# Order of tile 0's gating, of the scale's load and of the softplus chain in a fused adapter and feed-forward kernel

## The chip, the cores and the metric

The kernel runs on one core of one Trainium2 chip. The metric is device time in microseconds from the start to the end of one execution. The engines are TensorE (PE, its weight loads PEld), VectorE (DVE), ScalarE (ACT), GpSimd (POOL) and SyncE (SP); each works through its own list of instructions in order, and they meet through semaphores.

## What is computed

Two layers follow each other, and x is added at the end. Shapes: x is 128 x 32 x 512 in float32; E = 8 experts of rank R = 16.

```python
base    = einsum('btd,od->bto', x, W)
logits  = einsum('btd,ed->bte', x, Wr) + onehot(lang_ids) * 5.0
topw, topi = top_k(logits, 2);  weights = softmax(topw)
gates   = sum(onehot(topi) * weights[..., None], axis=-2)
h       = einsum('btd,erd->bter', x, A)
cond    = base + 2.0 * einsum('bter,bte,eor->bto', h, gates, B)
out     = x + einsum('bsi,io->bso', cond, sign) * softplus(scale)
```

The kernel folds the two layers into one matrix: M = W^T · sign · softplus(scale) + identity, and B2 = B · sign · 2·softplus(scale). Then out = x·M + (gated h)·B2.

## The kernel before

**Numbers in two parts.** Each float32 operand is split into a high part (rounded by a copy to the fp32r type) and a low part (the operand less its high part). A product is three matmuls: high·high, high·low, low·high. High parts are mostly ACT copies, low parts are subtractions on DVE or POOL.

**The start.** PE runs 18 warm-up matmuls (L577) and then M from W and sign, in four slices j of each (`high_high`, `low_high`, `high_low`, L589, L596, L603, the last slice at L569 to L571). The list of PE is fixed: `high_high(0)`, `low_high(0)`, `high_high(1)`, `high_low(0)`, and so on. `low_high(0)` waits for w_lo of slice 0. ACT issues the four loads of sign (L330), loads its function table (L332), and makes w_hi (L335) and sign_hi of slices 1 to 3 (L340). DVE makes sign_hi of slice 0 (L437) and all four w_lo (L422). POOL fills the identity blocks (L284) and makes all four sign_lo (L293). SP loads W, x of tile 0, the scale (L245), A, B, and x of tiles 1 and 2.

**Before the tiles.** DVE takes -|scale| (L443), transposes x of tile 0 (L432), and runs the rest of softplus as eight small dependent instructions (L448 to L457), between which ACT takes exp (L356) and ln (L358). Then come A and Wr transposed (L461, L464), m_full = p_m · softplus + eye (L470), and the low parts of the heads (Wr and A, L481 and L483) and of b (L487). PE makes p_b2 from b's parts (L626, L630); b2_hi is ACT's (L375), b2_lo is DVE's (L501, in `low_b2`).

**The tiles.** There are 32, one per time step, with three sets of buffers. For a tile, DVE transposes x (`turn_x`, L432), ACT makes xt_hi (`high_x`, L348), POOL makes xt_lo (`low_x`, L300), and PE multiplies them with `wide`, which holds the logits, the 128 columns of h, and M (L643; tile 0 at L668). DVE then gates: logits plus bias (L516), the largest (L524), their places (L532), a cast (L537), the denominator from ACT's exp (L540), `second` (L542), a reciprocal (L545), `gate` (L547) and h_gated (L551). PE transposes h_gated (`turn_h`, L686), ACT and DVE split it (ht_hi L381, ht_lo L507), and PE adds its product with b2 in the middle of a later tile's matmuls (`lora`, L679). The work is skewed: `step` s of PE multiplies tile s, adds the lora of tile s-2 in its middle, and ends with `turn_h` of tile s-1. In DVE's and ACT's step s the gating is of tile s-1, ht's parts are of tile s-2, and the transpose and the high part are of tile s+2. DVE's step 0 holds the transpose of x of tile 2 and then `low_b2`. In step 1 the transpose of tile 3's x (x3) stands in the middle of tile 0's gating, between the largest and their places, as it does in every later step.

Of the kernel before, what the change touches and what calls it, by code (L numbers as in the profile page):

```python
# [4 lines left out]
FP32 = mybir.dt.float32  # L5
# [7 lines left out]
P = 128  # L13
# [5 lines left out]
def adaln_ffn_kernel(nc: bass.Bass, x, lang_ids, W, Wr, A, B, sign, scale, out):  # L19
# [38 lines left out]
    with ctx:  # L58
# [138 lines left out]
        def slot(r, d=0):  # L197
            return (r + d) % S3
# [20 lines left out]
        def has(s, d):  # L219

            return s is None or 0 <= s + d < TILES

        @block.sync
        def _(sp_eng):
# [19 lines left out]
            load(0, 0, 0)  # L244
            sp_eng.dma_start(scale_in[:, :], scale.partition_broadcast(P)).then_inc(scale_loaded, 16)  # L245
            for i in range(NQ):
# [80 lines left out]
        def _(act):  # L327

            for j in range(OC):
                act.dma_start(sign_in[:, j, :], sign_load[:, j, :]).then_inc(sign_loaded[j], 16)  # L330

            nc.scalar.preload_act_table_set("natural_log_exp_and_others")  # L332
            for j in range(OC):
                act.wait_ge(w_loaded[j], 16)
                nc.scalar.activation(w_hi[:, j, :, :, :],  # L335
                                     w_in[:, j, :].rearrange("p (i k a) -> p k i a", i=NQ, k=KC),
                                     ACT.Copy).then_inc(w_hi_made, 1)
                if j >= EARLY:
                    act.wait_ge(sign_loaded[j], 16)
                    nc.scalar.activation(sign_hi[:, j, :], sign_in[:, j, :], ACT.Copy).then_inc(sign_hi_made, 1)  # L340

            def high_x(q, r, d, first=False):
# [9 lines left out]
            for i in range(NQ):  # L352
                act.dma_start(wr_in[Q * i:Q * i + E, :], wr_load[i, :, :]).then_inc(wr_loaded, 16)
            act.dma_start(ids_in[:, :], lang_ids.rearrange("(p a) -> p a", a=1)).then_inc(ids_loaded, 16)
            act.wait_ge(neg_abs_made, 1)
            nc.scalar.activation(exp_neg[:, :], sp[:, 0:1], ACT.Exp).then_inc(exp_neg_made, 1)  # L356
            act.wait_ge(exp_neg_made, 1)
            nc.scalar.activation(ln_one[:, :], exp_neg[:, :], ACT.Ln, bias=1.0).then_inc(ln_one_made, 1)  # L358
            high_x(0, 0, 0, first=True)
            act.wait_ge(head_turned, 1)  # L360
            nc.scalar.activation(wide_hi[:, :, E:HEAD].rearrange("p j (g b) -> p g j b", g=NQ), at[:, :, :, :],
                                 ACT.Copy).then_inc(head_hi_made, 1)
            act.wait_ge(head_turned, 2)
            nc.scalar.activation(wide_hi[:, :, 0:E], wrt[:, :, 0:E], ACT.Copy).then_inc(head_hi_made, 1)
            act.wait_ge(b_loaded, 16 * OC)
            nc.scalar.activation(b_hi[:, :, :, :], b_in[:, :, :, :],
                                 ACT.Copy).then_inc(b_hi_made, 1)
            for k in range(KC):
# [36 lines left out]
        def _(dve):  # L405
# [29 lines left out]
            for j in range(EARLY):  # L435
                dve.wait_ge(sign_loaded[j], 16)
                nc.vector.tensor_copy(sign_hi[:, j, :], sign_in[:, j, :]).then_inc(early_sign_hi_made, 1)  # L437
                low_w(j)
            for j in range(EARLY, OC):
                low_w(j)  # L440

            dve.wait_ge(scale_loaded, 16)
            nc.vector.tensor_scalar(sp[:, 0:1], scale_in[:, :], -1.0, scale_in[:, 0:1], ALU.mult, ALU.min)\  # L443
                .then_inc(neg_abs_made, 1)
            turn_x(0, 0, 0, first=True)

# [10 lines left out]
            nc.vector.tensor_scalar(sp[:, 11:12], sp[:, 10:11], SCALING, None, ALU.mult).then_inc(softplus_made, 1)  # L457
            softplus = sp[:, 10:11]

            dve.wait_ge(a_loaded, 16 * NQ)  # L460
# [12 lines left out]
            def low_m(k):  # L473
# [4 lines left out]

            fold(0)
            dve.wait_ge(head_hi_made, 2)  # L480
            nc.vector.tensor_tensor(wide_lo[:, :, 0:E], wrt[:, :, 0:E], wide_hi[:, :, 0:E].bitcast(FP32),  # L481
# [3 lines left out]
                                    ALU.subtract).then_inc(head_lo_made, 1)  # L485
            dve.wait_ge(b_hi_made, 1)
            nc.vector.tensor_tensor(b_lo[:, :, :, :], b_in[:, :, :, :],  # L487
                                    b_hi[:, :, :, :].bitcast(FP32), ALU.subtract).then_inc(b_lo_made, 1)
            fold(1)
# [7 lines left out]
            def low_b2():  # L497

                dve.wait_ge(bias_made, 1)
                dve.wait_ge(b2_hi_made, 1)  # L500
                nc.vector.scalar_tensor_tensor(b2_lo[:, :], p_b2[:, :], sp[:, 11:12], b2_hi[:, :].bitcast(FP32),  # L501
                                               ALU.mult, ALU.subtract).then_inc(b2_lo_made, 1)
# [7 lines left out]
            def step(q, r, s):  # L510
                done = S3 * q + r
                n = slot(r, -1)
                if has(s, -1):

                    dve.wait_ge(head_ready, done)
                    nc.vector.tensor_tensor(logits[:, :], pair[n][0][:, 0:E], bias[:, :], ALU.add)\  # L516
                        .then_inc(logits_made, 1)
                    dve.wait_ge(logits_made, done)
# [4 lines left out]
                if has(s, -1):  # L523
                    nc.vector.max(top[:, :], logits[:, :]).then_inc(top_made, 1)  # L524
                    dve.wait_ge(top_made, done)
                if s == 0:
                    turn_x(q, r, LEAD, first=True)
                    low_b2()
                elif has(s, LEAD):
                    turn_x(q, r, LEAD, first=(s is not None and s + LEAD < S3))  # L530
# [4 lines left out]
                if has(s, -1):  # L535
# [18 lines left out]
                        gate[:, :].unsqueeze(2).to_broadcast([P, E, R]), ALU.mult, ALU.mult)\  # L554
                        .then_inc(h_gated_made, 1)
                if s == TILES - 1 + LAG:

# [210 lines left out]
```

## Time and profile before

| | |
|---|---|
| time, median of 3 runs | 165.2 us (165.15 to 165.34) |
| time of the profiled execution | 164.64 us |
| its span, first to last instruction | 162.8 us |
| TensorE clock granted, mean share | 0.997 |
| busy: PE, DVE, ACT, POOL | 158.3, 97.6, 66.0, 52.1 us |

The profiled execution lies 0.56 us below the median of the runs, and 1.84 us of its time are outside its span. Positions below are microseconds from the start of the span. A timeline row gives start and length; a merged row (x4) gives the first start and the stretch to the last end. In brackets stands the idle time of the engine ahead of the row and what ended it. The names b_lo and pair stand for several tensors whose numbers are left out: b_lo at L501 is b2_lo.

### The profile page before, as it was taken

How to read it: one execution, taken by the hardware profiler on the slowest of the kernel's cores; microseconds unless marked ns; L12 is line 12 of the kernel's file. 1: busy time of each engine (PE TensorE's matmuls, PEld its weight loads, DVE VectorE, ACT ScalarE, POOL GpSimd, SP SyncE). 2: the span in 40 equal slices, each digit the busy share in tenths (PEclk: the TensorE clock that was granted, in tenths of full speed). 3: DMA queues.
4: the chain of work that ended last, by engine and by line, in shares of the span. 5: the costliest groups of instructions: out<-in, count | busy, mean ns of one | idle time of the engine just before them, and what ended most of it. 6: DMA issues, size and time to landing. Idle time of an engine off the chain costs nothing.

```text
span 162.8 us, 3711 instructions
## 1 busy us (share of the span) xinstructions
PE 158.3 (97%) x1070; PEld 153.8 (94%) x1070; DVE 97.6 (60%) x416; ACT 66.0 (41%) x177; POOL 52.1 (32%) x50
## 2 busy tenths in 40 slices
PE   7999998999999999999999999999999999999993
PEld 5788897999999999999999999999999999999992
DVE  5689997555556665554554555556665555455741
ACT  3654722434344333344444343344333344443440
POOL 2994453332222233333333322222333333333000
PEclk9999999999999999999999999999999999999998
DMA  4996323424333333334333333333333333111113
GB/s 170 380 146 136 90 82 101 131 70 146 105 122 114 124 119 115 124 129 129 129 129 127 104 101 117 112 121 123 113 123 120 128 129 129 64 64 64 68 66 129
DMA packets 29431, 19.51 MB, mean 120 GB/s; under 512 B 7248, under 2 KB 24432, under 8 KB 29424
## 3 DMA queue, kind: packets, MB, share of 16 engines
q1 hardware_dynamic: 28496, 18.23, 36.5%
q10 hardware_dynamic: 928, 1.20, 2.0%
q8 instruction: 3, 0.05, 0.1%
q14 instruction: 4, 0.03, 0.1%
HBM read 11.03 MB, written 8.39 MB: 119 GB/s over the span
## 4 chain that ended last, share of the span: by engine, by line
PE 90%; DVE 7%; issue 1%; ACT 0%; DVEq 0%
PE pair L643 66%; PE pair L679 14%; PE p_b L577 2%; PE p_ht L686 2%; PE pair L589 2%; DVE m_full L470 2%; PE pair L596 2%; PE pair L603 2%; DVE xt L432 1%; DVE wide_lo L476 1%; DVE gate L547 1%; DVE b_lo L501 0%; DVE b_lo L487 0%; DVE wide_lo L483 0%; ACT y L395 0%
## 5 line engine op out<-in xcount | busy, mean ns | idle before, releaser
L300 POOL TENSOR_TENSOR xt_lo<-xt,xt_hi 128x512 fp32r<-128x512 f32 x32 | 41.6, 1299 | 91.5 <-ACT xt_hi L348 91.5
L643 PE MATMUL pair<-wide_hi,xt_hi 128*128 128x392 f32 (+1 forms) x248 | 60.8, 321 | 0.0
L643 PE MATMUL pair<-wide_hi,xt_lo 128*128 128x392 f32 (+1 forms) x248 | 58.3, 311 | 0.0
L643 PE MATMUL pair<-wide_lo,xt_hi 128*128 128x392 f32 (+1 forms) x248 | 58.3, 311 | 0.0
L643 PEld LDWEIGHTS pair<-wide_hi,xt_lo 128*128 128x128 f32 x248 | 38.6, 188 | 0.0
L643 PEld LDWEIGHTS pair<-wide_lo,xt_hi 128*128 128x128 f32 x248 | 38.5, 188 | 0.0
L643 PEld LDWEIGHTS pair<-wide_hi,xt_hi 128*128 128x128 f32 x248 | 38.3, 189 | 0.1
L394 ACT ACTIVATE y<-pair 128x256 f32<-128x256 f32 x31 | 11.9, 384 | 44.3 <-PE pair L679 44.3
L516 DVE TENSOR_TENSOR logits<-pair,bias 128x8 f32<-128x8 f32 x32 | 5.3, 165 | 35.7 <-PE pair L643 35.7
L432 DVE STREAM_TRANSPOSE xt<-x_in 128x512 f32<-128x512 f32 x32 | 22.7, 710 | 3.7 <-DVE top L524 3.2
L348 ACT ACTIVATE xt_hi<-xt 128x512 fp32r<-128x512 f32 x32 | 20.3, 633 | 2.8 <-DVE xt L432 2.8
L381 ACT ACTIVATE ht_hi<-p_ht 128x128 fp32r<-128x128 f32 x32 | 8.9, 277 | 22.6 <-PE p_ht L686 22.6
L507 DVE TENSOR_TENSOR ht_lo<-p_ht,ht_hi 128x128 fp32r<-128x128 f32 x32 | 9.3, 290 | 13.6 <-ACT ht_hi L381 13.6
L385 ACT ACTIVATE e<-top 128x1 f32<-128x1 f32 x32 | 9.5, 296 | 14.4 <-DVE top L524 14.3
L551 DVE SCALAR_TENSOR_TENSOR h_gated<-pair,rdenom,gate 128x128 f32<-128x128 f32 x32 | 11.2, 350 | 3.3
L679 PE MATMUL pair<-b_hi,ht_hi 128*128 128x256 f32 x64 | 13.0, 281 | 0.0
L679 PE MATMUL pair<-b_lo,ht_hi 128*128 128x256 f32 x64 | 12.9, 280 | 0.0
L679 PE MATMUL pair<-b_hi,ht_lo 128*128 128x256 f32 x64 | 12.8, 279 | 0.0
L395 ACT ACTIVATE y<-pair 128x256 f32<-128x256 f32 x32 | 12.2, 380 | 1.4 <-PE pair L679 1.4
L679 PEld LDWEIGHTS pair<-b_hi,ht_hi 128*128 128x128 f32 x64 | 9.9, 188 | 0.1
L679 PEld LDWEIGHTS pair<-b_lo,ht_hi 128*128 128x128 f32 x64 | 9.9, 188 | 0.0
L679 PEld LDWEIGHTS pair<-b_hi,ht_lo 128*128 128x128 f32 x64 | 9.8, 188 | 0.0
(82 smaller groups left out, 142.0 us busy)
## 6 DMA issues: line engine op xcount, KB each, us to landing
x_in<-in_x SPq DMA_DIRECT2D x128, 64.0 KB, 1.9
out<-y SPq DMA_DIRECT2D x31, 256.0 KB, 2.1
sign_in<-in_L_ffn_sign ACTq DMA_DIRECT2D x4, 256.0 KB, 5.1
w_in<-in_L_cond_W SPq DMA_DIRECT2D x4, 256.0 KB, 4.9
a_in<-in_L_cond_A SPq DMA_DIRECT2D x4, 64.0 KB, 5.1
b_in<-in_L_cond_B SPq DMA_DIRECT2D x4, 64.0 KB, 4.2
out<-y SPq DMA_DIRECT2D x1, 128.0 KB, 1.7
out<-y ACTq DMA_DIRECT2D x1, 128.0 KB, 1.8
```

What stands on the lines that cost most here:

```text
L300: nc.gpsimd.tensor_tensor(xt_lo[n][:, :, :].rearrange("p j (g b) -> p g j b", g=NQ), xt[n][:, :, :, :], xt_hi[n][:, :, :].bitcast(FP32).re ...
L348: nc.scalar.activation(xt_hi[n][:, :, :].rearrange("p j (g b) -> p g j b", g=NQ), xt[n][:, :, :, :], ACT.Copy).then_inc(xt_hi_made, 1)
L381: nc.scalar.activation(ht_hi[:, :], p_ht[:, 0:P], ACT.Copy).then_inc(ht_hi_made, 1)
L385: nc.scalar.activation(e2[:, :], top[:, 0:1], ACT.Exp, bias=top[:, 1:2], scale=-1.0)\
L394: nc.scalar.activation(y[n][:, 0:Y0], pair[n][0][:, HEAD:HEAD + Y0], ACT.Copy)
L395: nc.scalar.activation(y[n][:, Y0:D], pair[n][1][:, 0:D - Y0], ACT.Copy).then_inc(y_copied, 1)
L432: nc.vector.transpose(xt[n][:, :, :, :].rearrange("p g j b -> p (g j b)"), x_in[n][:, :, :].rearrange("p g c -> p (g c)")).then_inc(xt_mad ...
L507: nc.vector.tensor_tensor(ht_lo[:, :], p_ht[:, 0:P], ht_hi[:, :].bitcast(FP32), ALU.subtract)\
L516: nc.vector.tensor_tensor(logits[:, :], pair[n][0][:, 0:E], bias[:, :], ALU.add)\
L551: nc.vector.scalar_tensor_tensor(h_gated[:, :].rearrange("p (e r) -> p e r", e=E), pair[n][0][:, E:HEAD].rearrange("p (e r) -> p e r", e=E ...
L643: last = nc.tensor.matmul(pair[n][bank][:, at0:at0 + hi - lo], l[:, k, :], w[:, k, lo:hi], start=(opens and k == 0 and l is xt_hi[n] and w ...
L679: last = nc.tensor.matmul(o, l[:, :], w[:, (0, Y0)[bank]:(Y0, D)[bank]], start=False, stop=stop, skip_group_check=True)
```

## The change

It moves instructions and adds none.

- The scale's load goes from SP's list (between x of tile 0 and A) to ACT's, between the loads of sign's slices 1 and 2.
- -|scale| is taken on DVE after w_lo of slice 1, exp and ln on ACT after sign_hi of slice 2, and the eight small softplus instructions on DVE stand between w_lo of slices 2 and 3. The transpose of tile 0's x follows w_lo of slice 3.
- b's high part (ACT) and low part (DVE) stand ahead of the heads' instead of behind them.
- `low_b2` leaves DVE's step 0, and the transpose of x3 leaves the middle of tile 0's gating; both stand after h_gated of tile 0, at the end of step 1. The wait for bias goes from `low_b2` to the head of step 1.

```diff
@@ sync
             load(0, 0, 0)
-            sp_eng.dma_start(scale_in[:, :], scale.partition_broadcast(P)).then_inc(scale_loaded, 16)
@@ scalar
                 act.dma_start(sign_in[:, j, :], sign_load[:, j, :]).then_inc(sign_loaded[j], 16)
+                if j == 1:
+                    act.dma_start(scale_in[:, :], scale.partition_broadcast(P)).then_inc(scale_loaded, 16)
...
+                if j == 2:
+                    act.wait_ge(neg_abs_made, 1)
+                    nc.scalar.activation(exp_neg[:, :], sp[:, 0:1], ACT.Exp).then_inc(exp_neg_made, 1)
+                    act.wait_ge(exp_neg_made, 1)
+                    nc.scalar.activation(ln_one[:, :], exp_neg[:, :], ACT.Ln, bias=1.0).then_inc(ln_one_made, 1)
...
             high_x(0, 0, 0, first=True)
+            act.wait_ge(b_loaded, 16 * OC)
+            nc.scalar.activation(b_hi[:, :, :, :], b_in[:, :, :, :],
+                                 ACT.Copy).then_inc(b_hi_made, 1)
@@ vector
-            for j in range(EARLY, OC):
-                low_w(j)
-
+            low_w(1)
             dve.wait_ge(scale_loaded, 16)
             nc.vector.tensor_scalar(sp[:, 0:1], scale_in[:, :], -1.0, scale_in[:, 0:1], ALU.mult, ALU.min)\
                 .then_inc(neg_abs_made, 1)
-            turn_x(0, 0, 0, first=True)
+            low_w(2)
...
             softplus = sp[:, 10:11]
+            low_w(3)
+            turn_x(0, 0, 0, first=True)
...
             def low_b2():
 
-                dve.wait_ge(bias_made, 1)
                 dve.wait_ge(b2_hi_made, 1)
...
+                if s == 1:
+                    dve.wait_ge(bias_made, 1)
...
-                if s == 0:
-                    turn_x(q, r, LEAD, first=True)
-                    low_b2()
-                elif has(s, LEAD):
+                if has(s, LEAD) and s != 1:
                     turn_x(q, r, LEAD, first=(s is not None and s + LEAD < S3))
...
+                if s == 1:
+                    low_b2()
+                    turn_x(q, r, LEAD)
```

DVE before, from the transpose of tile 2's x to the head of tile 1's gating:

```order
L432 STREAM_TRANSPOSE xt<-x_in 128x512
L501 SCALAR_TENSOR_TENSOR b_lo<-p_b,sp,b_hi 128x512
L516 TENSOR_TENSOR logits<-pair,bias 128x8
L524 MAX top<-logits 128x8
L432 STREAM_TRANSPOSE xt<-x_in 128x512
L532 MAX_INDEX top_at<-top,logits 128x8
L537 CAST top_no<-top_at 128x2
L540 TENSOR_SCALAR denom<-e 128x1
L542 TENSOR_SCALAR second<-expert_no,top_no,e 128x8
L545 RECIPROCAL rdenom<-denom 128x1
L547 SCALAR_TENSOR_TENSOR gate<-expert_no,top_no,second 128x8
L551 SCALAR_TENSOR_TENSOR h_gated<-pair,rdenom,gate 128x128
```

The same stretch of DVE now:

```order
L434 STREAM_TRANSPOSE xt<-x_in 128x512
L519 TENSOR_TENSOR logits<-pair,bias 128x8
L527 MAX top<-logits 128x8
L532 MAX_INDEX top_at<-top,logits 128x8
L537 CAST top_no<-top_at 128x2
L540 TENSOR_SCALAR denom<-e 128x1
L542 TENSOR_SCALAR second<-expert_no,top_no,e 128x8
L545 RECIPROCAL rdenom<-denom 128x1
L547 SCALAR_TENSOR_TENSOR gate<-expert_no,top_no,second 128x8
L551 SCALAR_TENSOR_TENSOR h_gated<-pair,rdenom,gate 128x128
L502 SCALAR_TENSOR_TENSOR b_lo<-p_b,sp,b_hi 128x512
L434 STREAM_TRANSPOSE xt<-x_in 128x512
```

Two instructions of 512 columns, b2_lo and the transpose of x3, moved from ahead of and inside tile 0's gating to behind it.

ACT before, at the start of the program:

```order
L330 DMA sign_in<-in_L_ffn_sign 128x512 x4
L332 ACT_TABLE_LOAD
L335 ACTIVATE w_hi<-w_in 128x512 x2
L340 ACTIVATE sign_hi<-sign_in 128x512
L335 ACTIVATE w_hi<-w_in 128x512
L340 ACTIVATE sign_hi<-sign_in 128x512
```

The same stretch of ACT now, up to the last w_hi:

```order
L329 DMA sign_in<-in_L_ffn_sign 128x512 x2
L331 DMA scale_in<-in_L_ffn_scale 128x1
L329 DMA sign_in<-in_L_ffn_sign 128x512 x2
L333 ACT_TABLE_LOAD
L336 ACTIVATE w_hi<-w_in 128x512 x2
L341 ACTIVATE sign_hi<-sign_in 128x512
L336 ACTIVATE w_hi<-w_in 128x512
L341 ACTIVATE sign_hi<-sign_in 128x512
L344 ACTIVATE exp_neg<-sp 128x1
L346 ACTIVATE ln_one<-exp_neg 128x1
L336 ACTIVATE w_hi<-w_in 128x512
```

One DMA issue was put ahead of the table load, and exp and ln ahead of the last slice's w_hi.

## Rows read from the trace of the kernel before

**Rows 1.** The page's part 1: busy time, share of the span, instructions

```profile
PE 158.3 (97%) x1070; PEld 153.8 (94%) x1070; DVE 97.6 (60%) x416; ACT 66.0 (41%) x177; POOL 52.1 (32%) x50
```

**Rows 2.** Waits of PE: who for whom, us in total, times, longest

```profile
PE p_ht L686 <- DVE h_gated L551: 0.7, 1, 0.7
```

**Rows 3.** Timeline of PE, ends of its steps 1 and 2: start, length

```profile
25.64 0.46 PE L643 MATMUL pair<-wide_hi,xt_lo 128*128 128x392 f32 x2
26.77 0.33 PE L686 MATMUL p_ht<-ident,h_gated 128*128 128x128 f32 x1 [0.67 <-DVE h_gated L551]
...
28.71 0.40 PE L679 MATMUL pair<-b_hi,ht_hi 128*128 128x256 f32 x2
...
30.92 0.46 PE L643 MATMUL pair<-wide_hi,xt_lo 128*128 128x392 f32 x2
31.22 0.27 PE L686 MATMUL p_ht<-ident,h_gated 128*128 128x128 f32 x1
...
33.11 0.40 PE L679 MATMUL pair<-b_hi,ht_hi 128*128 128x256 f32 x2
```

**Rows 4.** Timeline of DVE, end of its step 0 to step 2

```profile
22.47 0.70 DVE L501 SCALAR_TENSOR_TENSOR b_lo<-p_b,sp,b_hi 128x512 fp32r<-128x512 f32 x1
23.10 0.14 DVE L516 TENSOR_TENSOR logits<-pair,bias 128x8 f32<-128x8 f32 x1
...
23.49 0.71 DVE L432 STREAM_TRANSPOSE xt<-x_in 128x512 f32<-128x512 f32 x1
...
24.98 1.28 DVE L547 SCALAR_TENSOR_TENSOR gate<-expert_no,top_no,second 128x8 f32<-128x8 f32 x1
26.36 0.35 DVE L551 SCALAR_TENSOR_TENSOR h_gated<-pair,rdenom,gate 128x128 f32<-128x128 f32 x1
...
27.51 0.29 DVE L507 TENSOR_TENSOR ht_lo<-p_ht,ht_hi 128x128 fp32r<-128x128 f32 x1 [0.73 <-ACT ht_hi L381]
```

**Rows 5.** The tile gate, whole span: duration ns min/median/max, first and last start

```profile
L547 DVE SCALAR_TENSOR_TENSOR gate<-expert_no,top_no,second x32: 225/227/1280, 25.0 to 156.9; 128x8 f32<-128x8 f32 x32
```

**Rows 6.** Timelines of POOL and of ACT beside tile 0's gating

```profile
23.29 1.30 POOL L300 TENSOR_TENSOR xt_lo<-xt,xt_hi 128x512 fp32r<-128x512 f32 x1 [1.92 <-ACT xt_hi L348]
24.94 1.29 POOL L300 TENSOR_TENSOR xt_lo<-xt,xt_hi 128x512 fp32r<-128x512 f32 x1 [0.35 <-ACT xt_hi L348]
...
27.13 0.28 ACT L381 ACTIVATE ht_hi<-p_ht 128x128 fp32r<-128x128 f32 x1 [2.27 <-PE p_ht L686]
```

**Rows 7.** Timeline of ACT at the start (ACTq: DMA issues)

```profile
0.73 1.86 ACTq L330 DMA_DIRECT2D sign_in<-in_L_ffn_sign  x4
2.62 1.28 ACT L332 ACT_TABLE_LOAD   x1 [2.62 <-issue]
4.18 0.63 ACT L335 ACTIVATE w_hi<-w_in 128x512 fp32r<-128x512 f32 x1 [0.28 <-DMA w_in<-in_L_cond_W]
```

**Rows 8.** Timelines of DVE and of POOL, slices 0 and 1

```profile
4.86 0.77 DVE L422 TENSOR_TENSOR w_lo<-w_in,w_hi 128x512 fp32r<-128x512 f32 x1
6.16 1.17 DVE L422 TENSOR_TENSOR w_lo<-w_in,w_hi 128x512 fp32r<-128x512 f32 x1 [0.54 <-ACT w_hi L335]
...
5.06 1.71 POOL L293 TENSOR_TENSOR sign_lo<-sign_in,sign_hi 128x512 fp32r<-128x512 f32 x1
```

**Rows 9.** Timelines of PE and of its weight loads: first slices, last slice

```profile
5.08 1.17 PE L589 MATMUL pair<-sign_hi,w_hi 128*128 128x512 f32 x4
6.08 1.07 PE L596 MATMUL pair<-sign_hi,w_lo 128*128 128x512 f32 x4
...
5.85 0.88 PEld L596 LDWEIGHTS pair<-sign_hi,w_lo 128*128 128x128 f32 x4
...
13.12 0.19 PEld L569 LDWEIGHTS pair<-sign_hi,w_hi 128*128 128x128 f32 x1
```

**Rows 10.** Tile sp in one window (DVE busy, ACT busy, PEclk, DMA, GB/s); DVE's last w_lo

```profile
11.48:13.27 1.79, 1.54 (x8) 0.00 (x0) 1.00 0.87 93
...
9.56 1.18 DVE L422 TENSOR_TENSOR w_lo<-w_in,w_hi 128x512 fp32r<-128x512 f32 x1 [0.53 <-ACT w_hi L335]
```

More of the change, by code:

```diff
@@ L354, in _ @@
             act.dma_start(ids_in[:, :], lang_ids.rearrange("(p a) -> p a", a=1)).then_inc(ids_loaded, 16)
[L355 to L358, printed above, removed]
             high_x(0, 0, 0, first=True)
+            act.wait_ge(b_loaded, 16 * OC)
+            nc.scalar.activation(b_hi[:, :, :, :], b_in[:, :, :, :],
+                                 ACT.Copy).then_inc(b_hi_made, 1)
             act.wait_ge(head_turned, 1)
@@ L364, in _ @@
             nc.scalar.activation(wide_hi[:, :, 0:E], wrt[:, :, 0:E], ACT.Copy).then_inc(head_hi_made, 1)
-            act.wait_ge(b_loaded, 16 * OC)
-            nc.scalar.activation(b_hi[:, :, :, :], b_in[:, :, :, :],
-                                 ACT.Copy).then_inc(b_hi_made, 1)
             for k in range(KC):
@@ L479, in _ @@
             fold(0)
+            dve.wait_ge(b_hi_made, 1)
+            nc.vector.tensor_tensor(b_lo[:, :, :, :], b_in[:, :, :, :],
+                                    b_hi[:, :, :, :].bitcast(FP32), ALU.subtract).then_inc(b_lo_made, 1)
             dve.wait_ge(head_hi_made, 2)
@@ L485, in _ @@
                                     ALU.subtract).then_inc(head_lo_made, 1)
-            dve.wait_ge(b_hi_made, 1)
-            nc.vector.tensor_tensor(b_lo[:, :, :, :], b_in[:, :, :, :],
-                                    b_hi[:, :, :, :].bitcast(FP32), ALU.subtract).then_inc(b_lo_made, 1)
             fold(1)
```

## Prediction

> **What bounds the kernel now.** I read the page's part 1 first: PE is busy 97% of the span [rows 1], so only what makes PE stand still, or start later, can change the time. Then the list of waits: from the first product to the last tile PE waits for another engine once, 0.7 us, its transpose of tile 0's h_gated for DVE [rows 2]; the list's other wait of PE is the warm-up's, for its zeros. Everything else that the change moves lies beside a busy PE and is worth nothing by itself, unless it makes a new wait.
>
> The timeline of PE sizes the one wait. At the end of step 1 the last pair of matmuls starts at 25.64, the transpose at 26.77, the first lora matmul of step 2 at 28.71. One step later, where nothing waits, the same three starts are 30.92, 31.22 and 33.11 [rows 3]. From the last pair to the lora that is 3.07 us against 2.19: **the stall costs 0.88 us**. Nothing later in the trace gives it back, since PE waits nowhere else.
>
> Why h_gated is late, from DVE's timeline: b2_lo stands ahead of the logits (22.47, so they start at 23.10), the transpose of x3 stands in the middle (23.49, 0.71 us), and `gate` takes 1.28 us [rows 4]. The other 31 gates take 225 to some 230 ns [rows 5]. The gate started at 24.98, 0.04 us behind POOL's xt_lo (24.94), and ended at 26.26, 0.03 behind POOL's end of 26.23 [rows 4, 6]: it stood until POOL's instruction was over. That xt_lo is x3's, which the transpose in the middle had set off. The first slices show the same: w_lo of slice 1 starts at 6.16 while POOL works on sign_lo (5.06, 1.71 us, to 6.77) and ends at 7.33, 0.56 after POOL; in its turn that sign_lo takes 1.71, since w_lo of slice 0 (from 4.86 to 5.63) was there first [rows 8]. A POOL subtraction with nothing in its way takes 1.30 [rows 6]. So of two such instructions the later stands still until the earlier is over.
>
> The Trainium skill (SBUF — State Buffer, "Who interferes with whom") states this as a lock: a DVE instruction with two SBUF inputs and a GpSimd instruction that reads SBUF share a port pair, and the one that issues second is blocked for the whole of the first. By that rule the gate's 1.28 us is a lost race and not work, and the trace agrees (0.03 us between the two ends).
>
> **The change part by part.**
>
> *Gating ahead of b2_lo and x3.* Logits take b2_lo's place, near 22.47; the largest, places, cast, `second` and the reciprocal follow with no transpose between. The gate is then due between 23.5 and 24.3 (24.98 less 0.63 for b2_lo and 0.71 for the transpose is 23.64; ACT's exp may hold it a little). There it meets another xt_lo of POOL, tile 2's, from 23.29 to 24.59 [rows 6], and stands until 24.62. h_gated starts 0.10 after the gate as before, and is done at 24.62 + 0.10 + 0.35 = 25.07 [rows 4]. PE wants it 0.30 after its last pair (30.92 to 31.22), at 25.94 [rows 3]: 0.87 us to spare, with the second stall counted. The whole 0.88 us goes.
>
> What is late next: b2_lo (0.70), x3's transpose (0.71), its high part on ACT (0.63, as w_hi [rows 7]), and behind that in ACT's list ht_hi of tile 0 (0.28), then DVE's ht_lo (0.10 + 0.29). End to end from 25.07 that is 27.78; DVE's instructions overlap their predecessors by 0.07 (23.10 against 23.17), so about 27.6. PE's lora wants it at 28.71 - 0.88 = 27.83, its weights a little sooner [rows 3, 4, 6]. Cost 0 to 0.15; I take 0. This is the thinnest cover behind the gating. x3's low part is needed one step later.
>
> *The scale's load on ACT.* SP gets free of one issue, which nobody waits for. On ACT it stands ahead of the table load. Four issues and the gap behind them take 2.62 - 0.73 = 1.89, 0.47 each, so the table load goes from 2.62 to 3.09 and ends at 4.37 instead of 3.90. The first w_hi, which had waited for its data until 4.18, starts at 4.37, **0.19 later**, and ends at 5.00 instead of 4.81 [rows 7]. Two things hang on it. First, PE's first product (5.08): it came 0.27 after w_hi's end, while h_gated's transpose came 0.06 after h_gated [rows 3, 4, 9]; with the short lag it starts where it did, with the long one 0.19 later; the warm-up matmuls cover most of it, so I take 0.06. Second, w_lo of slice 0: it started 0.05 after w_hi's end and would now start at 5.05. POOL's sign_lo of slice 0 starts at 5.06 [rows 8], held by sign_hi and the identity fills, which don't move. Before, w_lo was 0.20 ahead; now it is a **dead heat**. The table load may let the next instruction in a little before its recorded end, as ordinary instructions do, and the issue may be some hundredths shorter; then w_lo is ahead. If it is, it ends by 5.05 + 0.77 = 5.82, and PE asks for it at 5.85, or 0.06 later with its own start: no stall [rows 8, 9].
>
> *Softplus between w_lo 2 and 3.* The eight small instructions take 1.79, and w_lo of slice 3, which started at 9.56, ends that much later at most: 10.74 + 1.79 = 12.53; PE's weights for the last slice are loaded at 13.12 [rows 9, 10]. Cost 0, with 0.6 to spare. Tile 0's transpose and the heads follow and are wanted only by the first tile. exp and ln on ACT (short ones, on one column) stand ahead of the last w_hi, which waits for its load anyway. The scale's packets now go ahead of sign's slices 2 and 3; those products are PE's seventh and later, so a few tenths there cost nothing.
>
> *b's parts ahead of the heads'.* The same instructions in another order on both engines; PE waits for neither before [rows 2], and the sum of their lengths ahead of the next m_full is unchanged. 0.
>
> **Sum.** -0.88 + 0.06 = -0.82 us, on the profiled 164.64 gives 163.8; the runs' median stands 0.56 above that execution, so 165.2 - 0.82 = **164.4 us**. Its own range, with 0 to 0.19 at the start and 0 to 0.15 at the lora, is 164.2 to 164.65.
>
> **The rivals.**
>
> *POOL is first at slice 0 (slower than before).* If w_lo of slice 0 comes behind sign_lo, POOL runs to 5.06 + 1.30 = 6.36, w_lo ends 0.56 later at 6.92, and PE's `low_high(0)`, the second product in its fixed list, gets its weights at 6.97. Before, they loaded at 5.85 and the first matmul ran at 6.08 [rows 8, 9]: PE loses between 0.89 and 1.12 us, and all later products shift with it, since none waits for a load by then. With the gain of 0.88 that is +0.01 to +0.24, so 165.2 to 165.45; I take 165.3. It decides when w_lo's start passes 5.06, that is when w_hi of slice 0 ends 0.20 later than before instead of 0.19. For it speaks that the sum lands within 0.02 us of the point; against it, that both uncertain terms more likely make ACT sooner than later, and that DVE took the port ahead of POOL's sign_lo when it had stood waiting.
>
> The Trainium skill's rule (SBUF — State Buffer, "Issue order, not op shape, decides who blocks") speaks against this part of the change: by it the 0.19 us on ACT is not worth 0.19 but either nothing or POOL's whole instruction.
>
> *The gating is not sooner.* Something else holds the logits or ACT's exp in step 1, or the wait for bias, or the lora of step 2 waits longer for ht_lo than the rows say. Then part of the 0.88 is only moved: 165.0, within 164.8 to 165.5. The rows give h_gated 0.87 us of slack, which speaks against it; the chain to ht_lo has hardly 0.2.
>
> **How the numbers follow.** Some 0.2% (0.33 us) is what a measurement of this kernel can tell from no change: faster means under 164.87, slower over 165.53. The forecast has 0.60; all of it is faster. POOL first has 0.31: 0.01 faster, 0.23 the same, 0.07 slower (its upper end with some loss at the lora besides). The gating not sooner has 0.09: 0.01 faster, 0.06 the same, 0.02 slower. Together 0.62, 0.29 and 0.09. The range must hold most of the first two, which are 0.9 us apart: 164.2 to 165.4. The likeliest alone has 164.2 to 164.65.
>
> **What would show it.** Right: in the new trace PE's list of waits has no h_gated; last pair to lora at the end of step 1 is near 2.2 us; tile 0's gate ends with tile 2's xt_lo; h_gated ends near 25.1; ACT's table load starts near 3.1 and w_hi near 4.4. The race is read from w_lo and sign_lo of slice 0: w_lo under 0.8 us long and sign_lo about 1.8 if DVE was first; w_lo about 1.9 and a wait of PE for w_lo near 6 us if POOL was. A wait of PE's lora for ht_lo near 27.7 would show the thin chain. Wrong would be any new wait of PE between the last slice and the first tile, or a gate of tile 0 that ends after 25.5.

## The result and the profile after

The changed kernel's median is **165.37 us** (165.12 to 166.86, 22 runs) against 165.0 (164.28 to 165.96, 22 runs) for the kernel before on the same chip: ratio 1.0041, 95% interval 1.0024 to 1.0059. It is a little slower. I had forecast 164.4, faster by 0.82; measured is 0.37 slower. The time lies inside the range, at its far end, within 0.1 us of what the rival "POOL is first at slice 0" was priced at.

The profiled execution is 165.87 us with a span of 164.1 (before 164.64 and 162.8); it stands 0.5 above its median, and the one before 0.36 below its own. So the two profiles lie 1.23 us apart where the medians lie 0.37 apart: what follows is the account of these two executions, and a usual run loses less. Part 1 of its page, to be held against [rows 1]:

```profile
PE 159.6 (97%) x1070; PEld 154.0 (94%) x1070; DVE 98.9 (60%) x416; ACT 65.8 (40%) x177; POOL 51.4 (31%) x50
```

PE has the same 1070 instructions and 97%. The waits of its weight loads (who for whom, us in total, times, longest) say more:

```profile
PEld pair L599 <- DVE w_lo L424: 0.7, 1, 0.7
PEld pair L671 <- DVE wide_lo L478: 0.6, 1, 0.6
PEld pair L592 <- ACT w_hi L336: 0.5, 1, 0.5
PEld pair L572 <- issue: 0.5, 1, 0.5
PEld pair L682 <- issue: 0.2, 1, 0.2
```

The one stall of before, the transpose of h_gated [rows 2], is gone. In its place PE waits for w_lo of slice 0 (L599), at the first tile for the low part of M (L671), at the last sign slice (L572, where the view names no releaser) and a little at the lora (L682). L592, the first product, had its wait of 0.5 before too.

The ledger is read from starts of the same instruction in both timelines of PE (us from the start of the span):

| first matmul of | before | after | after minus before |
|---|---|---|---|
| first product | 5.08 | 5.08 | 0 |
| second product (w_lo 0) | 6.08 | 6.94 | +0.86 |
| third product | 7.00 | 7.98 | +0.98 |
| last sign slice | 13.34 | 14.56 | +1.22 |
| first tile (step 0) | 18.78 | 20.10 | +1.32 |
| step 1 | 22.38 | 24.26 | +1.88 |
| transpose of h_gated | 26.77 | 27.83 | +1.06 |
| lora of step 2 | 28.71 | 29.85 | +1.14 |

So the gating gave back 0.82 (1.88 to 1.06), and the losses ahead of it outweigh that: 0.98 at slice 0, 0.24 more up to the last slice, 0.10 up to the first tile, 0.56 in the first tile; 0.08 more comes at the lora. Not all of them come of the change: most of the 0.56 is found without it, as the part on why the prediction was wrong shows.

PE at the end of step 1, which answers to [rows 3]:

```profile
27.53 0.46 PE L646 MATMUL pair<-wide_hi,xt_lo 128*128 128x392 f32 x2
27.83 0.27 PE L689 MATMUL p_ht<-ident,h_gated 128*128 128x128 f32 x1
```

The transpose follows the last pair by 0.30 as where nothing waits, and the lora comes 29.85 - 27.53 = 2.32 behind that pair, against 3.07 before and 2.19 undisturbed.

ACT, DVE, POOL and PE's weight loads at slice 0, which answer to [rows 7 to 9]:

```profile
3.10 1.28 ACT L333 ACT_TABLE_LOAD   x1 [3.10 <-issue]
4.40 0.63 ACT L336 ACTIVATE w_hi<-w_in 128x512 fp32r<-128x512 f32 x1
...
5.06 1.83 DVE L424 TENSOR_TENSOR w_lo<-w_in,w_hi 128x512 fp32r<-128x512 f32 x1 [0.39 <-ACT w_hi L336]
5.07 1.27 POOL L292 TENSOR_TENSOR sign_lo<-sign_in,sign_hi 128x512 fp32r<-128x512 f32 x1
6.94 0.76 PEld L599 LDWEIGHTS pair<-sign_hi,w_lo 128*128 128x128 f32 x4 [0.72 <-DVE w_lo L424]
```

Two subtractions start 0.01 apart; POOL's takes its plain 1.27 us, DVE's 1.83 instead of 0.77, and ends 0.55 behind POOL's end. PE's weights are 1.09 later than before (5.85 to 6.94).

### The profile page after: what moved, and what is told of

Same layout as the page of the kernel before. It is cut to its first block, busy times and chain, and to the rows that moved or that the text cites. A ratio compares the mean times of both kernels' runs of the same rounds, so it can differ in the third digit from the quotient of the medians.

```text
span 164.1 us, 3711 instructions
## 1 busy us (share of the span) xinstructions
PE 159.6 (97%) x1070; PEld 154.0 (94%) x1070; DVE 98.9 (60%) x416; ACT 65.8 (40%) x177; POOL 51.4 (31%) x50
## 3 DMA queue, kind: packets, MB, share of 16 engines
q10 hardware_dynamic: 1072, 1.20, 2.3%
## 4 chain that ended last, share of the span: by engine, by line
PE 84%; SPq 7%; DVE 4%; DMA 2%; ACT 1%; issue 1%
PE pair L646 67%; PE pair L682 14%; SPq L249 3%; PE p_ht L689 2%; DMA b_in<-in_L_cond_B 2%; DVE wide_lo L478 2%; SPq L246 1%; DVE m_full L472 1%; SPq L227 1%; SPq L243 1%; DVE b_lo L483 0%; ACT b_hi L363 0%; DVE wide_lo L488 0%; DVE xt L434 0%; PE pair L671 0%
## 5 line engine op out<-in xcount | busy, mean ns | idle before, releaser
L682 PE MATMUL pair<-b_hi,ht_hi 128*128 128x256 f32 x64 | 13.0, 282 | 0.0
L682 PE MATMUL pair<-b_lo,ht_hi 128*128 128x256 f32 x64 | 12.9, 281 | 0.0
L682 PE MATMUL pair<-b_hi,ht_lo 128*128 128x256 f32 x64 | 12.9, 279 | 0.0
L542 DVE TENSOR_SCALAR second<-expert_no,top_no,e 128x8 f32<-128x8 f32 x32 | 10.2, 317 | 0.0
L682 PEld LDWEIGHTS pair<-b_hi,ht_hi 128*128 128x128 f32 x64 | 9.8, 188 | 0.3 <-issue 0.2
L682 PEld LDWEIGHTS pair<-b_lo,ht_hi 128*128 128x128 f32 x64 | 9.9, 188 | 0.0
```

The lines of the kernel that those rows point to most:

```text
L542: nc.vector.tensor_scalar(second[:, :], expert_no[:, :], top_no[:, 1:2], e2[:, 0:1], ALU.is_equal, ALU.mult).then_inc(second_made, 1)
L682: last = nc.tensor.matmul(o, l[:, :], w[:, (0, Y0)[bank]:(Y0, D)[bank]], start=False, stop=stop, skip_group_check=True)
```

## The experiments

The theory with which I began: PE lost at slice 0 because the dead heat went to POOL, and the rest stood as I had it. The rival: the scale's load between the sign slices slows the loads themselves. The differences below are medians, each against the kernel before on the same chip.

| run | us | before | difference | ratio, 95% |
|---|---|---|---|---|
| changed_again | 166.17 | 165.01 | +1.16 | 1.0023 to 1.009 |
| gating_alone | 164.25 | 165.01 | -0.76 | 0.9924 to 0.9985 |
| gating_again | 164.23 | 164.68 | -0.45 | 0.9947 to 0.9999 |
| start_alone | 166.41 | 165.01 | +1.40 | 1.0056 to 1.011 |
| pool_waits_for_w_lo | 165.53 | 165.01 | +0.52 | 1.0009 to 1.0062 |
| pool_waits_b_last | 165.27 | 164.77 | +0.50 | 1.0016 to 1.0056 |
| sign_in_five | 165.61 | 164.77 | +0.84 | 1.003 to 1.0064 |
| ids_between_slices | 165.82 | 164.77 | +1.05 | 1.0041 to 1.0095 |
| scale_twice | 166.32 | 164.68 | +1.64 | 1.0067 to 1.014 |
| scale_on_sp_first | 164.45 | 164.77 | -0.32 | 0.9969 to 1.0006 |
| scale_behind | 165.02 | 164.68 | +0.34 | 1.0009 to 1.006 |
| scale_behind_pool_waits | 164.81 | 164.68 | +0.13 | 0.998 to 1.0032 |

**The two halves.** changed_again is the changed kernel once more, on another chip. Its loads fall to 105 and 99 GB/s from 5 to 7 us, so the low rate (below) is no accident of one execution.

> The changed kernel once more, on the same chip as the other runs of this set. Theory (lost port race): 0.1 to 0.6 us over the kernel before; w_lo of slice 0 about 1.85 us long, PE's weights for the second product near 6.95. Second theory (tiny packets): between 5 and 7.5 us of the span the DMA engines move under 200 GB/s again and the later slices of W and sign land one to two us later than before; if the low rate in the first profile was an accident of that execution, they move near 390 GB/s.

gating_alone is the kernel before with these lines of the diff and no others (gating_again is the same kernel, later):

```diff
-                dve.wait_ge(bias_made, 1)      # in low_b2
+                if s == 1:
+                    dve.wait_ge(bias_made, 1)  # at the head of step
-                if s == 0:
-                    turn_x(q, r, LEAD, first=True)
-                    low_b2()
-                elif has(s, LEAD):
+                if has(s, LEAD) and s != 1:
...
+                if s == 1:
+                    low_b2()
+                    turn_x(q, r, LEAD)         # behind h_gated
```

> The kernel before with the gating part of the change alone: b2_lo and x3's transpose behind tile 0's h_gated, the wait for bias at the head of step 1; the start is as before. If the gating's price was right, 0.88 us faster than before (164.1 where before has 165.0), no wait of PE for h_gated, nothing new at the lora. If the gain is taken back by the chain to ht_lo, 0.7 or less and a wait of PE's lora near 27.7.

> The kernel before with the gating part alone, once more, beside the three others on one chip: 0.7 to 0.9 us under before again. It is the measure for the kernel with the scale behind the slices and POOL's wait: if the rest of the change is harmless there, the two agree within 0.2 us.

start_alone is the changed kernel with just these lines put back.

> The kernel before with all of the change but the gating: scale on ACT, softplus between w_lo 2 and 3, b's parts ahead of the heads'. Lost port race alone: 0.9 to 1.1 us slower than before. With tiny packets that slow the loads besides: 1.3 us or more, and new waits of PE between 13 and 24 us.

The gating is worth 0.76 and 0.45, both intervals below 1, the second less than the 0.7 to 0.9 that I expected; everything else in the change costs 1.40. The two do not add up to changed_again to the tenth (0.64 against 1.16), which is within what the three intervals leave. DVE and PE in gating_again show how the stall went:

```profile
23.91 1.10 DVE L540 TENSOR_SCALAR second<-expert_no,top_no,e 128x8 f32<-128x8 f32 x1
...
25.38 0.35 DVE L549 SCALAR_TENSOR_TENSOR h_gated<-pair,rdenom,gate 128x128 f32<-128x128 f32 x1
26.06 0.46 PE L644 MATMUL pair<-wide_hi,xt_lo 128*128 128x392 f32 x2
26.36 0.27 PE L687 MATMUL p_ht<-ident,h_gated 128*128 128x128 f32 x1
...
28.38 0.48 PE L680 MATMUL pair<-b_hi,ht_hi 128*128 128x256 f32 x2
```

h_gated ends at 25.73, and PE takes it at 26.36, 0.30 behind its last pair. The lora stands 2.32 behind that pair, exactly as in the changed kernel.

start_alone's profile holds a surprise: with the same program at the start as the changed kernel, DVE won there.

```profile
5.07 0.69 DVE L424 TENSOR_TENSOR w_lo<-w_in,w_hi 128x512 fp32r<-128x512 f32 x1 [0.39 <-ACT w_hi L336]
```

POOL's two sign_lo start at 5.08 in that execution. The heat really is dead: it fell to POOL in the profiles of after and changed_again and to DVE here. And start_alone was still slow, in this very execution too (166.40, where its median is 166.41), so the race is not the only loss.

**The race by itself.** sign_in_five is the kernel before with a fifth DMA issue on ACT ahead of the table load: slice 3 of sign comes in two large pieces, and nothing else is moved.

```diff
-                act.dma_start(sign_in[:, j, :], sign_load[:, j, :]).then_inc(sign_loaded[j], 16)
+                for c in ((0, D),) if j < OC - 1 else ((0, Y0), (Y0, D)):
+                    act.dma_start(sign_in[:, j, c[0]:c[1]], sign_load[:, j, c[0]:c[1]]).then_inc(sign_loaded[j], 16)
...
-                    act.wait_ge(sign_loaded[j], 16)
+                    act.wait_ge(sign_loaded[j], 16 if j < OC - 1 else 32)
```

> The kernel before with the last slice of sign loaded by two DMAs instead of one: ACT has one more issue ahead of its table load, and no small packet is added. Theory of two losses: the race at slice 0 is lost (w_lo of slice 0 about 1.85 us long, PE's weights for the second product near 6.95), the loads keep near 390 GB/s from 3 to 7 us, and the time is 0.9 to 1.1 us over before. If the low rate comes of any fifth issue on ACT, the loads fall under 200 GB/s here too and the loss is larger.

DVE and PE in its profile:

```profile
5.21 1.70 DVE L423 TENSOR_TENSOR w_lo<-w_in,w_hi 128x512 fp32r<-128x512 f32 x1 [0.53 <-ACT w_hi L336]
6.96 1.19 PE L597 MATMUL pair<-sign_hi,w_lo 128*128 128x512 f32 x4 [0.53 <-DVE w_lo L423]
```

An issue on ACT is enough: w_lo, 0.14 behind POOL's start here, is blocked, PE's second product comes at 6.96 (before 6.08), and the median rises by 0.84, though w_lo starts only 0.35 us later (4.86 to 5.21). The Trainium skill (SBUF — State Buffer, "Who interferes with whom") says that whoever issues first gets the shared port pair for its whole instruction and the other is blocked. The trace agrees: w_lo ends 0.55 behind POOL's sign_lo, which stands from 5.07 to 6.36.

**The race taken away.** pool_waits_for_w_lo is the changed kernel with one wait more, ahead of POOL's first sign_lo; pool_waits_b_last also puts b's two instructions behind the heads' again, on ACT and DVE.

```diff
+                    pool.wait_ge(w_lo_made, 1)
```

> The changed kernel with one more wait: POOL's first sign_lo waits for DVE's first w_lo, so that DVE is always first at slice 0. If the lost race is all of the loss, 164.2 where before has 165.0 (the forecast of 0.82 less), and PE loads the second product's weights near 5.9. If slow loads cost besides, between 164.4 and 165.2, with waits of PE behind the slices.

> The changed kernel with POOL's wait for the first w_lo and with b's parts behind the heads' again, as before. If b's place costs when b lands late, the wait of PE in the first tile (0.6 us in the run with POOL's wait) goes and the time is 0.2 to 0.5 under that run's; if the late softplus and w_lo of slice 3 set that wait, the time is the same.

The rival theory gained here. With the second product on time (6.13) and h_gated on time, the kernel should have been 0.8 faster than before; it is 0.52 slower, more than I had allowed either theory. From its timelines of ACT and PE:

```profile
9.99 0.63 ACT L342 ACTIVATE sign_hi<-sign_in 128x512 fp32r<-128x512 f32 x1 [1.55 <-DMA sign_in<-in_L_ffn_sign]
14.17 0.47 PE L573 MATMUL pair<-sign_hi,w_hi 128*128 128x512 f32 x1 [0.41 <-DVE w_lo L425]
23.46 0.56 PE L672 MATMUL pair<-wide_lo,xt_hi 128*128 128x392 f32 x2 [0.29 <-DVE wide_lo L479]
```

ACT waits 1.55 us for slice 2 of sign, which it found loaded in the kernel before; PE's last slice starts at 14.17 instead of 13.34, and the first tile waits as it did after. Where b's parts stand makes no difference that can be seen (+0.50 against +0.52, on two chips).

**The small packets by themselves.** ids_between_slices is the kernel before plus one load that nothing uses, in the place where the change puts the scale's: the 128 words of lang_ids, one to a partition, which brings the packets of ACT's queue from 928 to 1072. scale_twice does the same with a second load of the scale, 128 copies of one word.

```diff
+                if j == 1:
+                    act.dma_start(probe_in[:, :], lang_ids.rearrange("(p a) -> p a", a=1)).then_inc(probe_loaded, 16)
```

> The kernel before with one more load, of which nothing is made: the 128 words of the ids, 4 bytes to a partition, on ACT between sign's slices 1 and 2; the scale stays on SP. If 128 packets of 4 bytes between the slices are enough, the loads fall under 200 GB/s between 5 and 7.5 us and sign's slices 2 and 3 land 1 to 3 us later, and it is slower than the five issues alone or as slow. If it takes the one address that the scale's 128 packets all read, the rate stays near 390 GB/s.

> The kernel before with one more load, of which nothing is made, as in the run with the ids, but of the scale: 128 packets of 4 bytes that all read one word, on ACT between sign's slices 1 and 2. If the one word makes it worse than 128 words: under 150 GB/s in 6 to 7 us where the ids left 273, and 0.2 us or more slower than that run's 1.05 us over before. If 128 small packets are all of it, the same rate and the same time.

Windows of 1 us (length, then busy time of PE, PEld, DVE, ACT, POOL, then PEclk, DMA share, GB/s). Before:

```profile
5.00:6.00 1.00, 0.99 (x5) 0.82 (x5) 0.62 (x1) 0.51 (x1) 1.00 (x2) 1.00 1.06 393
6.00:7.00 1.00, 1.00 (x7) 0.79 (x6) 0.84 (x1) 0.65 (x2) 1.00 (x2) 1.00 1.05 404
```

After:

```profile
5.00:6.00 1.00, 0.99 (x3) 0.82 (x3) 0.94 (x1) 0.78 (x3) 1.00 (x2) 1.00 0.50 119
6.00:7.00 1.00, 0.71 (x4) 0.24 (x2) 1.00 (x2) 0.40 (x1) 0.86 (x2) 1.00 0.51 123
```

sign_in_five, a fifth issue with large packets:

```profile
5.00:6.00 1.00, 0.77 (x3) 0.67 (x4) 0.79 (x1) 1.00 (x3) 1.00 (x2) 1.00 1.03 365
6.00:7.00 1.00, 0.47 (x3) 0.04 (x1) 1.00 (x2) 0.33 (x1) 0.96 (x2) 1.00 1.01 383
```

ids_between_slices, 128 packets of 4 B:

```profile
5.00:6.00 1.00, 0.91 (x4) 0.77 (x5) 0.76 (x2) 0.78 (x3) 1.00 (x2) 1.00 0.76 242
6.00:7.00 1.00, 1.00 (x6) 0.83 (x5) 1.00 (x1) 0.49 (x2) 1.00 (x2) 1.00 0.91 273
```

scale_twice, the same packets, all of one word:

```profile
5.00:6.00 1.00, 0.98 (x3) 0.81 (x3) 0.93 (x1) 0.87 (x3) 1.00 (x2) 1.00 0.53 170
6.00:7.00 1.00, 0.90 (x4) 0.37 (x3) 1.00 (x2) 0.32 (x1) 0.95 (x2) 1.00 0.42 90
```

The last column is the reading. A fifth issue with large pieces, which brings ACT's queue to 1072 packets too, leaves the rate near 375; half a kilobyte in 128 packets brings it from 400 to between 90 and 270 for two microseconds. All profiles say the same of these two windows: the seven without small packets among the sign slices have 287 to 406 GB/s in them, the seven with such packets 76 to 273. W's slice 2, on SP's queue, comes later too in the changed kernel and in scale_twice (ACT takes it at 8.35 and 7.89, before at 7.16), but not with the ids (6.92). In ids_between_slices ACT waits 1.97 us for slice 2 of sign, and PE's weight loads 1.2 us for b_hi:

```profile
9.53 0.63 ACT L345 ACTIVATE sign_hi<-sign_in 128x512 fp32r<-128x512 f32 x1 [1.97 <-DMA sign_in<-in_L_ffn_sign]
17.11 0.50 PE L631 MATMUL p_b<-sign_hi,b_hi 128*128 128x512 f32 x1 [0.74 <-ACT b_hi L371]
```

The race was not lost in that profile (second product at 6.12), so what it lost goes by late data; it stands 0.41 above its median, and how many of the usual runs, with five issues on ACT, lose the race besides isn't known. scale_twice lost the race as well (6.95), so the difference of the two, 0.6 us, doesn't tell whether one word costs more than 128: the rate is lower with one word (90 against 273), yet ACT begins slice 2 of sign at about the same time (9.57 and 9.53).

**The scale's load put elsewhere.** scale_on_sp_first is the changed kernel with that load on SP again, between W and x. scale_behind keeps it on ACT, behind the last sign slice; scale_behind_pool_waits adds POOL's wait to that.

```diff
-                if j == 1:
+                if j == OC - 1:
                     act.dma_start(scale_in[:, :], scale.partition_broadcast(P)).then_inc(scale_loaded, 16)
```

> The changed kernel with the scale's load on SP, behind W and ahead of x: ACT has its four issues as before, and no small packet stands between the slices. If the scale's load on ACT is the whole loss (race and slow loads), this is as fast as the gating alone, 0.7 to 0.9 us under before. If the softplus order or b's order cost by themselves, between that and before, with a wait of PE at the last slice or in the first tile.

> The changed kernel with the scale's load behind sign's slice 3, and without POOL's wait: the race is lost, and no packet is among the slices. The prediction's rival as it was priced: 0.0 to 0.3 us over before, PE's weights for the second product near 6.95, and no new wait of PE at the last slice. If it is as slow as the changed kernel (0.4 to 1.1 over), the packets' place was not the cause.

> The changed kernel with the scale's load behind sign's slice 3 in ACT's list instead of behind slice 1, and with POOL's wait for the first w_lo: as many issues ahead of the table load, the same 128 packets, but no slice behind them in ACT's queue, and no race at slice 0. If the two losses are the race and the packets among the slices, both are gone: 0.6 to 0.9 us under before, loads near 390 GB/s from 5 to 7 us. If the softplus order costs by itself, waits of PE at the last slice stay and it is within 0.3 us of before.

scale_behind in the same windows:

```profile
5.00:6.00 1.00, 0.81 (x3) 0.65 (x3) 0.76 (x1) 0.83 (x3) 1.00 (x2) 1.00 1.03 395
6.00:7.00 1.00, 0.93 (x5) 0.42 (x3) 1.00 (x2) 0.58 (x2) 0.75 (x2) 1.00 1.07 406
```

Full rate again, and PE's only new waits are at slice 0 (second product 6.95) and 0.2 at the lora: this is the rival much as I had priced it, +0.01 to +0.24, measured +0.34 with an interval from +0.15. scale_on_sp_first has neither ACT's issue nor the packets among the sign slices; the -0.32 (its interval just takes in no change) should have been about -0.8, and PE waits at the first tile:

```profile
14.01 1.30 POOL L300 TENSOR_TENSOR xt_lo<-xt,xt_hi 128x512 fp32r<-128x512 f32 x1 [1.93 <-ACT xt_hi L353]
14.73 1.13 DVE L482 TENSOR_TENSOR b_lo<-b_in,b_hi 128x512 fp32r<-128x512 f32 x1
22.21 0.57 PE L670 MATMUL pair<-wide_lo,xt_hi 128*128 128x392 f32 x2 [0.23 <-DVE wide_lo L477]
```

With x0's transpose behind the last w_lo, POOL's xt_lo of tile 0 falls beside DVE's subtractions of b and the heads, and b_lo takes 1.13 us instead of 0.68. That is the least part of the wait: from the first tile to step 1 PE takes 4.07 us here (3.60 before), and 4.00 in gating_again, where none of this is moved. In scale_behind_pool_waits both remedies are in, but the scale comes so late that DVE stands for it ahead of w_lo 2:

```profile
9.97 0.21 DVE L444 TENSOR_SCALAR sp<-scale_in 128x1 f32<-128x1 f32 x1 [2.16 <-DMA scale_in<-in_L_ffn_scale]
13.88 0.47 PE L573 MATMUL pair<-sign_hi,w_hi 128*128 128x512 f32 x1 [0.28 <-DVE w_lo L425]
```

PE's last slice waits then (13.88), and the result can't be told from no change. No place that I tried for the early scale is seen to gain more than the gating alone; the -0.32 of scale_on_sp_first and the -0.45 of gating_again, on two chips, can't be told apart. The version that clearly beats both kernels is gating_alone, 164.25 and 164.23 us.

## Why the prediction was wrong

In the sum the gating stood for -0.88 and the whole start for +0.06. Run apart, the gating gives -0.76 and -0.45, and the start costs +1.40 (start_alone). So the forecast failed at the start, in the steps named below.

**What bounds the kernel, and the gating: right.** h_gated no longer holds PE. Of the 0.88, 0.75 is seen between the last pair and the lora (3.07 to 2.32), in the changed kernel and in gating_again alike; the medians of the gating alone give 0.76 and 0.45. The other 0.13 stays at the lora, within my 0 to 0.15, of which I took 0. One detail was off: I had the gate stand behind POOL's xt_lo of tile 2, and it was the instruction two ahead of it.

```profile
25.18 1.29 POOL L299 TENSOR_TENSOR xt_lo<-xt,xt_hi 128x512 fp32r<-128x512 f32 x1 [1.92 <-ACT xt_hi L354]
25.38 1.10 DVE L542 TENSOR_SCALAR second<-expert_no,top_no,e 128x8 f32<-128x8 f32 x1
...
26.85 0.35 DVE L551 SCALAR_TENSOR_TENSOR h_gated<-pair,rdenom,gate 128x128 f32<-128x128 f32 x1
```

`second` ends at 26.48, POOL at 26.47. h_gated ends at 27.20, 0.63 ahead of PE's need at 27.83, where I had 0.87 to spare. One stall takes the place of the other, so the result is the same.

**The dead heat: the first step that failed.** The 0.47 per issue, the table load near 3.09 and w_hi near 4.37 came out to 0.03 us. PE's first product moved by nothing, so the 0.06 that I took for it was 0. But I let DVE win with two chances in three, because the table load "may let the next instruction in a little before its recorded end". It didn't: the load ended at 4.38, w_hi started at 4.40, w_lo at 5.06, POOL at 5.07. The loss, 0.86 at the second product and 0.98 at the third, lies within the rival's 0.89 to 1.12 or just under; sign_in_five alone measures 0.84. Two starts within 0.01 us can't be ranked from a profile; start_alone shows them falling the other way. But the race doesn't add to the next loss: where DVE won or was made to win, PE's last slice still starts at 14.40 (start_alone) and 14.17 (pool_waits_for_w_lo), against 14.56 here and 13.34 before. Of the 0.98, only 0.2 to 0.4 is left by then; the rest lies under what the late data cost.

**The scale's packets: the second step that failed,** and enough without the race, as start_alone's +1.40 shows. I wrote that they go ahead of sign's slices 2 and 3 and that "a few tenths there cost nothing". I priced the issue on ACT and the order in the queue, but not what the packets do to the queues' rate. In the kernel before, the same load stood on SP behind W and x, and landed 5.8 us after its issue. ACT after, beside [rows 7]:

```profile
8.35 0.63 ACT L336 ACTIVATE w_hi<-w_in 128x512 fp32r<-128x512 f32 x1 [1.95 <-DMA w_in<-in_L_cond_W]
10.38 0.63 ACT L341 ACTIVATE sign_hi<-sign_in 128x512 fp32r<-128x512 f32 x1 [1.40 <-DMA sign_in<-in_L_ffn_sign]
11.25 0.62 ACT L336 ACTIVATE w_hi<-w_in 128x512 fp32r<-128x512 f32 x1
16.10 0.64 ACT L363 ACTIVATE b_hi<-b_in 128x512 fp32r<-128x512 f32 x1 [0.51 <-DMA b_in<-in_L_cond_B]
```

Before, the first of these ran at 7.16, the second at 7.70 and the third at 8.90. So W's slice 2 is taken 1.2 and sign's slice 2 2.7 us late, not tenths; W's slice 3, 2.35 late, stands behind exp. Loads vary without small packets too, but less: ACT takes W's slice 3 at 9.81 and 9.47 in the two profiles of the gating alone.

**Softplus between w_lo 2 and 3, "cost 0, with 0.6 to spare": failed for the same reason.** The 0.6 was cover for slices that land on time. Now exp stands behind sign_hi of slice 2, w_hi 3 behind exp, and DVE's eight small instructions end at 12.93; w_lo 3 then meets POOL:

```profile
12.47 1.29 POOL L292 TENSOR_TENSOR sign_lo<-sign_in,sign_hi 128x512 fp32r<-128x512 f32 x1
12.84 1.46 DVE L424 TENSOR_TENSOR w_lo<-w_in,w_hi 128x512 fp32r<-128x512 f32 x1
14.56 0.47 PE L572 MATMUL pair<-sign_hi,w_hi 128*128 128x512 f32 x1
```

w_lo 3 ends at 14.30 instead of 10.74, and the last slice, by then 0.98 late, starts 0.24 later still. With the loads on time and no race lost, as in scale_on_sp_first, w_lo 3 ends at 12.63 (my working said 12.53) and the last slice comes 8.27 behind the first product, as before (8.26). So the step was sound on the condition that it didn't state.

**The first tile, "0" for b's parts and x0's transpose: the cover was not looked at, and the order is not the main cause.** I argued that the sum of DVE's work ahead of the next m_full is unchanged. It is, but the waits and the neighbours are not, and there was next to nothing to spare: DVE's last low part of M ended at 21.92 before, and PE began step 1 at 22.38, 0.46 behind; after, where PE waited for it, the two are 23.80 and 24.26, 0.46 apart too. DVE after:

```profile
16.77 0.74 DVE L483 TENSOR_TENSOR b_lo<-b_in,b_hi 128x512 fp32r<-128x512 f32 x1 [0.41 <-ACT b_hi L363]
18.15 2.06 DVE L472 SCALAR_TENSOR_TENSOR m_full<-pair,sp,eye 128x512 f32<-128x512 f32 x3
20.75 3.05 DVE L478 TENSOR_TENSOR wide_lo<-m_full,wide_hi 128x512 fp32r<-128x512 f32 x3
```

b_lo waits for b's late load with the heads and the folds behind it; the folds start at 18.15 (before 16.27) and the low parts at 20.75 (18.88), 1.87 later where PE was 1.32 late. The 0.56 at the first tile is that difference. But it can't be put down to the change: gating_again, whose start is that of the kernel before, has 0.40 of it (4.00 us from the first tile to step 1 against 3.60), and gating_alone 0.39. DVE's first fold, m_full, before and in gating_again, and the scale there:

```profile
14.30 0.75 DVE L470 SCALAR_TENSOR_TENSOR m_full<-pair,sp,eye 128x512 f32<-128x512 f32 x1 [0.22 <-PE pair L571]
```

```profile
11.31 0.21 DVE L443 TENSOR_SCALAR sp<-scale_in 128x1 f32<-128x1 f32 x1 [0.30 <-DMA scale_in<-in_L_ffn_scale]
...
14.66 0.71 DVE L470 SCALAR_TENSOR_TENSOR m_full<-pair,sp,eye 128x512 f32<-128x512 f32 x1
```

Before, DVE was 0.22 ahead of PE at the first fold. In gating_again it waited for a scale that landed later, and was not. This parts all fourteen profiles: where the first fold waits for PE (before, sign_in_five, scale_behind), step 1 comes 3.59 to 3.61 us behind the first tile; in the eleven others 3.99 to 4.21. scale_behind has all of the change's order and no such wait, so the order alone doesn't make it. With the order before the loss is 0.39 to 0.43 (four profiles), with the new one, whole or in part, 0.47 to 0.61 (seven): some 0.2 at most is left for the order and for late loads of b. How often a usual run of the kernel before pays the 0.4, its one profile can't say. Nor does b's own place decide it: with the heads first, in pool_waits_b_last, the small low part of the heads takes 0.68 us instead of 0.18 beside POOL's xt_lo of tile 0, which x0's later transpose has brought there, and PE waits as long. With b on time, in scale_on_sp_first, it is b_lo that meets POOL.

**The rivals.** "POOL is first" came true in the profile, and its 165.3 is near the 165.37. That is luck in part: with the race removed the kernel is still half a microsecond slower than before, and the 165.3 was reckoned from a before of 165.2 (three runs), which is 165.0 over 22; the measured +0.37 lies above that rival's +0.01 to +0.24. "The gating is not sooner" fell. One sum of the forecast was off too: its own range has a low end of 164.2, and its terms give 165.2 - 0.88 = 164.3.

What stays open: how often the dead heat falls to either side in the runs without a profile; how much of the packets' cost a usual run has, since the changed kernel lost 0.37 us on one chip and 1.16 on another; whether 128 copies of one word are worse than 128 words, which was not tried with the race taken out; and why the small packets lower the rate.

## What to carry to other kernels

When a step is moved, cost its DMAs by what they do to the transfers in flight beside them, not by their bytes: half a kilobyte in 128 packets, put among slices of 256 KB, cost 1.05 us with its issue (ids_between_slices), more than the 0.45 to 0.76 that the gating gave. Where a sum lands within hundredths of a race, give the two outcomes even chances, and count on a cover only after asking whether its data still come on time, in more than one profile. A part that gains by itself, as the gating does, is worth running alone before it is bundled with others.

## What the runs showed of the hardware

128 packets of 4 B between large loads on ACT's queue took the rate of all loads together from about 400 GB/s to between 76 and 273 for some two microseconds, in all seven profiles that had them there. A fifth load that was made of large pieces left it at 365 to 383.

A TENSOR_SCALAR on 128x8 was held by POOL's subtraction to its end (1.10 us against 0.29 where it is not), though it has a single tensor of eight columns as input and scalars beside it. The Trainium skill (SBUF — State Buffer, "Who interferes with whom") lists `tensor_scalar` among the operations that can enter a two-port mode and then contend with GpSimd, when their operands meet its conditions. The trace agrees (`second` ends 0.01 us behind POOL's instruction), and I had applied the rule to instructions with two tensors only.

Two instructions that start 0.01 us apart by the profile can be ranked either way: DVE is recorded first at 5.06 and 5.07 in the two cases, and lost the first and won the second.
